# Two blocks instead of four in the second batch of looked-up blocks of a three-layer graph network, with the input read and measured earlier

## What is computed

```
h = relu(layernorm(x))
for layer in 0, 1, 2:
    agg = segment_sum(h[src], dst) / max(count(dst), 1)      # mean over a node's incoming edges
    h   = agg @ Wl.T + bl + h @ Wr.T
    if layer < 2: h = relu(batch_norm(h) * gamma + beta)     # over the 6250 nodes
out = x + log_softmax(h)
```

## Time and profile before

| | us |
|---|---|
| median of 3 runs | 1455.91 (1454.22 to 1457.84) |
| profiled execution, its time | 1454.64 |
| its span in the trace | 1452.8 |
| PE busy | 1350.9 (93%) |
| DVE busy | 556.4 (38%) |
| ACT busy | 541.4 (37%) |
| POOL busy | 565.1 (39%) |

### The profile page before, as it was taken

How to read it: one execution, slowest core, us unless ns; L and a number is a source line. 1 busy time by engine, 2 the same in 40 slices (tenths; PEclk the granted TensorE clock), 3 DMA queues, 4 the chain that set the end, 5 groups by cost and what they waited for, 6 DMA issues and landing times.

```text
span 1452.8 us, 31402 instructions
## 1 busy us (share of the span) xinstructions
PE 1350.9 (93%) x13681; PEld 835.5 (58%) x13681; DVE 556.4 (38%) x1019; ACT 541.4 (37%) x898; POOL 565.1 (39%) x562
## 2 busy tenths in 40 slices
PE   1399999999999999999999999999999899999996
PEld 1277777777777776544554545545548654444444
DVE  6977777686868763301010001100101212221223
ACT  4897878788787865500000000000000520000011
POOL 3423141404032100056566565556560025676640
PEclk9999999999999999999999999999999999999998
DMA  5334554535455542856656665665541688998982
GB/s 164 98 150 158 193 196 185 194 128 190 183 206 189 192 181 53 279 199 216 215 168 222 222 212 175 216 210 191 202 153 40 181 302 298 327 324 317 325 288 73
DMA packets 91986, 291.13 MB, mean 200 GB/s; under 512 B 17538, under 2 KB 53012, under 8 KB 88612
## 3 DMA queue, kind: packets, MB, share of 16 engines
q1 hardware_dynamic: 63596, 228.73, 43.9%
q0 software_dynamic: 21824, 55.44, 12.4%
q10 hardware_dynamic: 6424, 4.88, 1.1%
HBM read 197.78 MB, written 91.22 MB: 199 GB/s over the span
## 4 chain that ended last, share of the span: by engine, by line
PE 79%; ACT 6%; DMA 5%; issue 3%; POOL 3%; DVE 3%; ACTq 0%; DVEq 0%; SPq 0%; POOLq 0%
PE bank L1575 27%; PE bank L1157 16%; PE cells L1575 12%; PE cells L1149 7%; PE bank L1172 4%; PE bank L1175 4%; DMA hots<-table,src_i 3%; POOL hots L518 2%; PE cells L1200 2%; PE bank L1578 2%; ACT ring L654 2%; ACT junk L602 2%; PE cells L1656 1%; DMA parts<-in_pairs_dram,last_i 1%; PE bank L1925 1%
## 5 line engine op out<-in xcount | busy, mean ns | idle before, releaser
L518 POOL DMA_INDIRECT hots<-table,src_i x444 | 420.0, 946 | 463.9 <-DMA table<-parts 194.5
L1575 PE MATMUL bank<-ring,parts 128*128 128x500 f16 x2058 | 460.9, 373 | 0.4 <-DVE parts L1630 0.4
L654 ACT CAST ring<-cells 128x980 f16<-128x980 f32 (+1 forms) x325 | 337.9, 1058 | 97.6 <-PE cells L1149 91.8
L1157 PE MATMUL bank<-ring,parts 128*128 128x250 f16 (+1 forms) x2450 | 318.7, 272 | 2.3 <-ACT ring L654 2.3
L1575 PEld LDWEIGHTS bank<-ring,parts 128*128 128x128 f16 x2058 | 192.1, 96 | 221.6 <-issue 9.7
L882 DVE TENSOR_TENSOR hots<-iotas,tab 128x980 f16<-128x980 f16 (+3 forms) x262 | 245.5, 997 | 5.3 <-ACT tab L618 5.3
L1157 PEld LDWEIGHTS bank<-ring,parts 128*128 128x128 f16 (+1 forms) x2450 | 216.2, 98 | 34.1 <-ACT ring L654 3.1
L1575 PE MATMUL cells<-ring,parts 128*128 128x500 f16 (+1 forms) x980 | 215.8, 373 | 0.0
L1710 ACT ACTIVATE Z<-bank,vec 128x250 f32<-128x250 f32 x48 | 19.9, 467 | 396.3 <-PE bank L1175 396.3
L1575 PEld LDWEIGHTS cells<-ring,parts 128*128 128x128 f16 (+1 forms) x980 | 90.7, 96 | 113.0 <-issue 9.7
L962 DVE BATCH_NORM_STATS2 st<-Z 128x6 f32<-128x250 f32 x96 | 35.5, 412 | 293.4 <-ACT Z L1710 263.4
(11 more groups left out here) (203 smaller groups left out, 855.9 us busy)
## 6 DMA issues: line engine op xcount, KB each, us to landing
ring<-c_blocks SPq DMA_DIRECT2D x120, 750.0 KB, 6.4
c_blocks<-ring SPq DMA_DIRECT2D x25, 3062.5 KB, 10.6
ring<-c_blocks SPq DMA_DIRECT2D x40, 812.5 KB, 6.5
rcb<-rc_row SPq DMA_DIRECT2D x69, 125.0 KB, 7.8
hots<-table,src_i POOLq DMA_INDIRECT x444
Z<-in_x_dram SPq DMA_DIRECT2D x4, 768.0 KB, 6.9
table<-parts SPq DMA_DIRECT2D x2, 1536.0 KB
table<-parts ACTq DMA_DIRECT2D x2, 1536.0 KB
```

What stands on the lines that cost most here:

```text
L518: pool.indirect_dma_start(out=got[layer][:, 5 * (r % NGOT) + i, :], out_offset=None, in_=tables[layer], in_offset=bass.IndirectOffsetOnAxi ...
L654: act.copy(blk[c % 2][:, :, :].rearrange("p a (d g) -> p a d g", d=GD)[:, :, :, GPS * i:GPS * i + n], cells[t % 2][:, :, 0:n * NA].rearran ...
L1157: return pe.matmul(bank[b][:, 0:BD], view[0:r, a, part, m * P:m * P + P], blk[s][0:r, a, :], start=(a, part) == (0, 0), stop=(a, part) == ...
L1575: ins = pe.matmul(bank[b][:, 0:2 * BD].rearrange("p (s d) -> p s d", s=2), lhs, ring[0:r, :, BD * a:BD * a + BD], start=(a, part) == (0, 0 ...
```

## The change

The batches become block 0; blocks 1 and 2; blocks 3 to 6; 7 to 10; and so on, with 23 and 24 as the last. That is eight batches where there were seven. The batch of blocks 3 to 6 must now be ready for step 39, so its stages, which follow batch 1 (q = 1, t0 = 13), have distances of their own; the later ones keep theirs. `TG` moves by six steps, since the last tables are made later.

The third and fourth quarter of `x` are loaded one right after the other. VectorE measures the third before block 0's tables and the fourth right after the first lookup, with the scales; ScalarE's square root moves from step 3 to step 1. The sum of counts over the batches that hold the blocks 19 to 22 is written so that one batch alone can hold them all.

```diff
-    batches = [(0, 1)]
+    batches = [(0, 1), (1, 3)]
...
     for q in range(1, len(batches)):
         t0 = NST * batches[q][0]
-        chores[t0 + 9] = ("count", q, 0)
+        at = {"count": 9, "sample": 11, "rows": 18, "row": 24, "windows": 31, "ends": 33, "shift": 37, "tile": 41, "place": 42,
+              "table": 46, "turn": 48}
+        if q == 1:
+            at = {"count": 6, "sample": 1, "rows": 5, "row": 8, "windows": 12, "ends": 13, "shift": 17, "tile": 21, "place": 22,
+                  "table": 23, "turn": 24}
...
-    TG = NST * (NB - 2)
+    TG = NST * (NB - 2) + 6
...
             x_load(2)
-            sp.wait_ge(d_win[0], 16)
             x_load(3)
...
                     if t == 1:
                         for b in range(*batches[1]):
                             act_row(1, b)
-                    elif t == 3:
                         act.wait_ge(v_lnvar, 1)
                         act.activation(rsx[:, 1, :], rsx[:, 2, :], ACT.Sqrt, bias=epsc[:, 0:1]).then_inc(a_lnstd, 1)
...
             dve_lnstats(1, own)
+            dve_lnstats(2, own)
             dve_shift(0, 0)
...
                     if t == 0:
-                        dve_lnstats(2, own)
+                        dve_lnstats(3, own)
+                        dve_lnscales(own, 1)
                     elif t == 2:
                         dve_windows(1, own)
-                        dve_lnstats(3, own)
-                        dve_lnscales(own, 1)
```

More of the change, by code:

```diff
@@ L79, in gnn_program @@
         t0 = NST * batches[q][0]
-        chores[t0 + 9] = ("count", q, 0)
+        at = {"count": 9, "sample": 11, "rows": 18, "row": 24, "windows": 31, "ends": 33, "shift": 37, "tile": 41, "place": 42,
[3 more added lines that the diff above has]
+                  "table": 23, "turn": 24}
+        chores[t0 + at["count"]] = ("count", q, 0)
         if q + 1 < len(batches):
             for k, c in enumerate(range(*batches[q + 1])):
[L83 to L88, removed]
+                for what in ("sample", "row", "shift", "turn"):
+                    chores[t0 + at[what] + k] = (what, q + 1, c)
+            for what in ("rows", "windows", "ends", "tile", "place", "table"):
+                chores[t0 + at[what]] = (what, q + 1, 0)
+    assert len(chores) == 2 * (batches[1][1] - 1) + 4 + len(batches) - 1 + 4 * (NB - batches[1][1]) + 6 * (len(batches) - 2)
     turn_step = {c: t for t, (what, _, c) in chores.items() if what == "turn"}
@@ L1093, in dve_layer0 @@
                         parts_at = [batches[q][0] + 1 for q in range(len(batches)) if loose_part(q)]
[L1094 to L1102, removed]
+                        for k in parts_at:
+                            if k == parts_at[0]:
+                                ins = dve.tensor_scalar(tot[:, NB + 1:NB + 2], tot[:, k:k + 1], -1.0, None, ALU.mult)
+                            else:
+                                ins = dve.tensor_tensor(tot[:, NB + 1:NB + 2], tot[:, NB + 1:NB + 2], tot[:, k:k + 1],
+                                                        ALU.subtract)
+                            if k == parts_at[-1]:
+                                ins.then_inc(v_tot, 1)
+                            else:
+                                ins.then_inc(v_own, 1)
+                                dve.wait_ge(v_own, own.up())
                         dve_norms(own)
```

## The result

| | before | changed |
|---|---|---|
| median | 1455.91 | 1477.03 (1475.55 to 1480.65, 5 runs) |
| profiled execution | 1454.64 | 1476.33 |
| its span | 1452.8 | 1474.6 |

The ratio is 1.0145 with a 95% interval of 1.013 to 1.016: slower by 21 us. Forecast were 1470.6 and a range of 1460 to 1477; the time lies 0.03 us beyond the range's upper end. The side was right, the size was a third short.

A forecast was written before the change was run, and what follows sets the result against it. TensorE, busy 93%, was taken to bound the kernel after a ramp led by VectorE and ScalarE. Ramp 1.6, steps 14 to 39 12.1, later +1.5 and -0.5 sum to +14.7 us: 1470.6 us, range 1460 to 1477.

The forecast's parts named there:

- What bounds the kernel: Whole kernel: a ramp, then a stretch where each us TensorE waits lengthens the run; step distance covers waits.
- (a): Steps before 39 mainly: lost lead between stages makes TensorE wait; 1470.6 us, own range 1464 to 1474; chance 50%.
- (b): From step 18 on: only ScalarE's queue counts, VectorE passes row and windows without TensorE noticing; 1462 us; chance 14%.
- (d): Up to step 39: work only changes places, ScalarE alone paces, -2 cancels the ramp's +1.6; 1456 us; chance 10%.
- (e): Ramp: VectorE has 1.8 us less table work, step 13 comes 2.3 sooner; 1453.6 us; chance 6%.
- (c): After the waits at steps 19 and 26: TensorE slows, costing up to 3.6 us more; 1474 us; chance 16%.
- The sum: Whole kernel: 1.6 + 12.1 + 1.5 - 0.5 = +14.7 us, giving 1470.6 us.
- Steps 14 to 19: Four samples there delay VectorE's row stage and the patterns of 19/20 behind it; step 19's cells +5.65 us.
- The ramp: Up to step 13: earlier measuring and later second-half gathers, less saved shifts and table work; +1.6 us, bounds -0.5 and +4.
- Steps 19 to 26: Last row on ScalarE at step 24, one step before windows on VectorE, delays patterns 26/27; +3.3 us.
- Steps 26 to 39: Gathers beside block 1's store delay the shifts and patterns 32/33, +1.3 us; late table, turn and patterns of step 39, +1.8.
- Afterwards: Behind step 39: first samples' copies paid in block 3, +1.5 us; last batch of two blocks, -0.5; layers 1 and 2 untouched.

The follow-up runs named there:

- e3: Changed kernel with the samples of blocks 3 to 6 moved right behind block 0's row; ratio 1.006 to the kernel before.
- e8: Changed kernel with the shifts of blocks 1 and 2 moved from steps 5 and 6 to 7 and 8; ratio 1.0142 to the kernel before.
- e2: Changed kernel with the input loaded and measured as in the kernel before, so only the batches change; ratio 1.0089 to the kernel before.
- e7: Changed kernel with never-read products of zeros put into TensorE's two long waits, after steps 18 and 25; ratio 1.0141 to the kernel before.
- e6: Changed kernel with block 1 stored only after the second-half gathers of blocks 3 to 6 have landed; ratio 1.0171 to the kernel before.
- e10: Kernel before with the samples of blocks 5 to 8 moved right behind block 0's row; ratio 0.9984 to the kernel before.
- e5: Changed kernel run again unaltered, as a reference; ratio 1.0169 to the kernel before.

## Why the prediction was right in its side and short in its size

**What bounds the kernel.** Right. "The distance in steps is the cover" is what the runs show of the largest losses: they stand where a stage was brought close behind what it waits for, and go when the two are parted (e3, with its samples out of the way, and e8). What is left of them is the price of gathers and of GpSimd's pair, below.

**Rivals.** The forecast (a) was the right mechanism. (b), ScalarE's queue alone, falls with the changed profile: it had VectorE pass the row stage unnoticed, and TensorE waits 4.48 us for the patterns behind it while VectorE waits 7.67. (d), work only changes places, and (e) fall with the time; though (e)'s idea that the smaller batch speeds up the ramp is true by 1.1 us (e2). (c) was half right: the clock does fall after the wait of step 19, but costs at most 0.4 us up to step 32 (e7) where up to 3.6 was put, because the steps it slows are not those that are waited for. Its reading that step 13 ran at a granted clock of 1.00 is not in the earlier trace rows, whose windows end before that step and begin after it, but holds: from 63.4 to 66 us it is 1.00.

**The sum.** Forecast were +14.7, and the span grew by 21.8. The difference is 2.5 on the ramp, 1.5 in steps 19 to 26, 2.5 in steps 26 to 39 and 2.4 in the layers 1 and 2, less 1.6 behind step 39 in layer 0. That the time lies only just outside the range owes something to this last one.

**Steps 14 to 19**, +5.65: measured +5.55, and e3 takes back 5.4.

**The ramp**, the step that failed first: "Step 13 thus comes at +3 - 0.6 - 0.8 - 0.2 ... = +1.6". (The terms give +1.4, a slip of 0.2.) Its early marks came as said: patterns 2/3 out at 33, a wait of 1.3 for TensorE's product (1.28), patterns 4/5 from 35.0 (34.78), and VectorE at the shift at about 37.7 where 37.9 was put. Then the wait was to end "about 40.5" and ended at 43.15. The gathers of the second halves start at 37.39, since those of the first halves (two, issued from 33.6 on) stand ahead of them in GpSimd's queue, one with 2.22 us instead of 0.94; that is 3.5 later than before, not the "2.2" put, so 1.3 of the wait's extra length. The other 1.3 is the landing: the shift starts 5.8 us after its gather's issue, where some 4.4 was taken. So 2.7 us are the wait's, and step 13's +4.1 is nearly the predicted 1.6 plus these. The upper bound of +4 had been worked out and then not taken. Why the landing took 5.8 stays open. Before, and in e3, the gather for block 1 was used 3.5 and 3.6 us after its issue, and it was the next one that landed late (5.6, issued at 36.13 before). In the changed kernel SyncE sends the counts' reciprocals (L426) at 37.70, right behind block 1's gather; before and in e3 they go out right behind block 2's. No run moved them.

**Steps 19 to 26**, +3.3: measured +4.8. It was taken that TensorE goes on at 1.33 a step and the last row ends at 90.7 (by the recorded clock, without the ramp's share). In the trace the steps after the wait take about 2 us each, the first row starts at 90.78 and the last at 95.68. That looks like rival (c)'s loss, but e7 takes the slow steps away and step 26 moves by 0.4 at most, with a wait for the row gather of 1.2 us now seen on ScalarE. What holds step 26 is thus, as far as e7 shows it, the chain from the row stage (82.29) through the gathers to ScalarE's rows, with copies between them; the sum followed TensorE instead. The split of the 1.5 us inside this chain was not tried further.

**Steps 26 to 39**, +3.1: measured +5.6, the second step that failed: "GpSimd issues four gathers of first halves in 113.61 + 1.25 - 108.79 = 6.1 us". They took 104.64 - 96.98 = 7.66, since the third and fourth issue last 1.48 and 2.00 us where 0.94 was counted. This accounts for the 1.4 that steps 26 to 32 lose beyond the forecast (13.53 us where 10.79 stood, +2.7 for +1.3), though no run shortened the issues. "I take 5" for the landing was right: the shift starts 5.2 us after its gather's issue. And there was no term for GpSimd's pair of L504, 6.31 us where in this batch before it took 3.47: steps 32 to 39 are +2.8 for +1.8. In e6, with a landing of 3.6 and a pair of 3.48, the two stretches are +1.2 and +1.8, the forecast's, though its issues take 7.66 too.

**Afterwards.** "+1.5" and "-0.5" came as -0.55 together: the 1.5 us of copies that block 3 was to pay didn't show. e10 puts what the kernel before pays for these samples at 1.0; in the changed kernel no run was made on that term. "Layers 1 and 2 are untouched" is wrong by 2.4 us in the profiled execution. About 0.9 of it is seen at the layer's beginning, where eight matmuls of 500 columns take longer:

```profile
578.01 3.52 PE L1580 MATMUL bank<-ring,parts 128*128 128x500 f16 x8 [0.41 <-DVE parts L1635]
```

where 2.61 stood before. The runs don't tie it to the change: the same kernel again (e5) has 2.84 there, e8 3.52, and e10, which is the kernel before but for the samples, 3.51. The granted clock goes with it: TensorE begins these products at 0.50 in both kernels, and is at 0.94 from 560.0 to 561.2 before, 1.4 us into them, while the changed kernel is still at 0.50 from 579.5 to 581.5. What decides when it rises stays open, as does the rest of the 2.4, and why e7's median lies 3.6 us below e5's with step 39 later in e7 (their intervals overlap).

## What to carry to other kernels

Where a search is staged over several engines, the number of steps between a stage and its user is the resource that is spent: a row stage of two operations of 0.17 us became a wait of 4.5 us on TensorE when it was set one step behind what it reads, and an edit that "only" halves a batch has to be read as an edit of these distances. When such an order is laid out, put the stage whose inputs are known early (here the samples) as early as there is idle time, before the distances behind it are touched. And where several gathers are issued in a row on one engine, go by the slow issues in the trace, 2.0 to 2.2 us, and not by one short series: on the ramp and before step 32 the second halves were issued 1.3 and 1.6 us later than the sum had them.

## What the runs showed of the hardware

A gather of 128 rows from DRAM landed 2.5 to 3.6 us after its issue with no store beside it and 7.2 to 9.6 beside the store of a block (the four first-half gathers in e6 and in the changed kernel). On the ramp, where no block is stored, second halves landed 5.2 and 5.6 us after their issue (38.64 in the changed kernel, 36.13 before). The issue on GpSimd took 0.94 us in most cases, 1.3 to 1.7 in some and 2.0 to 2.2 in others, within one series of four.

The same pair of operations on GpSimd (L504, 256 columns) took 3.47 us before, 3.48 in e6, and 6.31 in the changed kernel, for the first batch prepared behind the ramp, always beside patterns on VectorE. It isn't the change's alone: the kernel before has one pair of 7.44 too, at 205 us. Where the pair took 3.5, the patterns beside it took 2.26 instead of 2.06: one of the two engines loses, not always the same. Three rows of VectorE show it, two of e6 beside GpSimd's 3.48:

```profile
111.06 2.26 DVE L888 TENSOR_TENSOR hots<-iotas,tab 128x2560 f16<-128x2560 f16 x2
...
113.70 2.25 DVE L888 TENSOR_TENSOR hots<-iotas,tab 128x2560 f16<-128x2560 f16 x2
```

and one of the changed kernel beside its 6.31:

```profile
112.60 2.07 DVE L885 TENSOR_TENSOR hots<-iotas,tab 128x2560 f16<-128x2560 f16 x2
```

The Trainium skill ("GPSIMD Engine Reference", §8 Key points) says that GpSimd shares its SBUF interfaces with VectorE and that they contend when VectorE reads two inputs from SBUF. The patterns do (`iotas` and `tab`), and the trace agrees: of the pair of 6.31 the operation beside the patterns took 5.16 us and the one behind them 1.07. Which of the two engines gives way no run here explains.
